# Gated cross-attention and a low-rank expert layer: the first two key groups by context blocks, in a new order of loads, with zeros in front

## What is computed

```python
x = x + tanh(g_xattn) * xattn(layernorm(x), ctx, ...)
x = x + tanh(g_ffn) * ffn(layernorm(x), ...)

# xattn(text, features)
features_n = rmsnorm(features, fn_w)
Q = rmsnorm(text @ Wq_w.T + Wq_b, qn_w)
K = rmsnorm(features_n @ Wk_w.T + Wk_b, kn_w)
attn = softmax(Q @ K.T / sqrt(1024))
attended = attn @ features_n

# ffn(x)
base = x @ W_base.T + b_base
w = normalized part of softmax(x @ W_gate.T) above its threshold
moe = 2.0 * sum over experts e of w_e * (x @ A_e.T) @ B_e.T
```

## Time and profile before

| | us |
|---|---|
| median of 3 executions | 489.45 (488.79 to 489.53) |
| the profiled execution | 489.19 |
| its span, first to last instruction | 487.1 |
| TensorE busy | 473.6 (97%) |
| VectorE busy | 345.9 (71%) |
| ScalarE busy | 164.6 (34%) |
| GpSimd busy | 127.5 (26%) |

### The profile page before, as it was taken

The page is one execution under the profiler, slowest core; times in us unless marked ns, Lnnn a source line. Parts: engine busy times, 40 slices in busy tenths (PEclk is TensorE's granted clock), DMA queues, the critical chain, the costliest instruction groups (busy, mean ns, idle before and its releaser), DMA issues.

```text
span 487.1 us, 6840 instructions
## 1 busy us (share of the span) xinstructions
PE 473.6 (97%) x2460; PEld 402.2 (83%) x2460; DVE 345.9 (71%) x720; ACT 164.6 (34%) x338; POOL 127.5 (26%) x113
## 2 busy tenths in 40 slices
PE   4999999999999999999999999999999999999997
PEld 3888899998888888888888887877888888888885
DVE  1267758563787867769977996988767679777742
ACT  3765312310214204227326325244151422414300
POOL 1011011002353353336152515514040401305000
PEclk9999999999999999999999999999999999999999
DMA  8962262027843368557669035040503113050202
GB/s 291 412 247 87 88 250 96 1 87 253 266 137 123 150 215 283 199 200 249 208 257 399 4 131 215 27 146 2 172 3 129 45 60 113 1 173 1 86 0 87
DMA packets 20160, 71.80 MB, mean 147 GB/s; under 512 B 2464, under 2 KB 3488, under 8 KB 18848
## 3 DMA queue, kind: packets, MB, share of 16 engines
q1 hardware_dynamic: 19984, 71.35, 40.8%
q10 hardware_dynamic: 144, 0.02, 0.0%
HBM read 56.69 MB, written 14.68 MB: 147 GB/s over the span
## 4 chain that ended last, share of the span: by engine, by line
PE 79%; DVE 11%; issue 4%; DMA 3%; ACT 2%; POOL 0%; SPq 0%; DVEq 0%; ACTq 0%; POOLq 0%
PE bank L706 8%; PE bank L710 8%; PE bank L708 8%; PE bank L558 6%; PE bank L623 6%; PE bank L625 6%; PE bank L624 6%; PE bank L588 3%; PE bank L590 3%; PE bank L589 3%; PE bank L686 3%; PE bank L487 2%; DVE wl_T L1316 2%; DMA out_dram<-xs 2%; PE bank L609 2%
## 5 line engine op out<-in xcount | busy, mean ns | idle before, releaser
L1430 POOL TENSOR_TENSOR small<-small,tiny 128x1 f32<-128x1 f32 (+2 forms) x25 | 23.6, 945 | 150.3 <-DVE small L1079 124.1
L623 PE MATMUL bank<-xth,gram 128*128 128x512 f32 x144 | 57.4, 398 | 0.0
L625 PE MATMUL bank<-xtl,gram 128*128 128x512 f32 x144 | 56.3, 391 | 0.0
L624 PE MATMUL bank<-xth,gram 128*128 128x512 f32 x144 | 56.1, 390 | 0.0
L1404 DVE SCALAR_TENSOR_TENSOR xs<-bank,tiny,xs 128x512 f32<-128x512 f32 x56 | 40.2, 747 | 21.6 <-PE bank L710 15.7
L706 PE MATMUL bank<-wh_B,zh 128*128 128x512 f32 x136 | 55.2, 406 | 0.0
L710 PE MATMUL bank<-wh_B,zl 128*128 128x512 f32 x136 | 53.5, 393 | 0.0
L708 PE MATMUL bank<-wl_B,zh 128*128 128x512 f32 x136 | 53.3, 392 | 0.0
L1458 POOL TENSOR_TENSOR sq_sum<-sq_sum,sq 128x512 f32<-128x512 f32 x24 | 32.0, 1332 | 62.7 <-DVE sq L1252 62.7
L1494 POOL TENSOR_TENSOR xs<-xs,bb 128x1024 f32<-128x1024 f32 x16 | 39.5, 2468 | 10.3 <-ACT zn L946 7.7
L706 PE MATMUL bank<-wh_T,zh 128*128 128x512 f32 x96 | 39.3, 410 | 1.8 <-DVE wl_T L1316 1.6
(11 more groups left out here) (185 smaller groups left out, 1111.5 us busy)
## 6 DMA issues: line engine op xcount, KB each, us to landing
xst<-x_dram SPq DMA_DIRECT2D x16, 512.0 KB, 3.6
xz<-xt_dram SPq DMA_DIRECT2D x16, 512.0 KB, 6.8
out_dram<-xs SPq DMA_DIRECT2D x14, 512.0 KB, 3.0
xa<-x_dram SPq DMA_DIRECT2D x12, 512.0 KB, 3.3
x<-xa SPq DMA_DIRECT2D x12, 512.0 KB, 2.6
xs<-x SPq DMA_DIRECT2D x12, 512.0 KB, 4.0
wq_raw<-wq_dram SPq DMA_DIRECT2D x8, 512.0 KB, 14.9
wr_B<-wb_dram SPq DMA_DIRECT2D x4, 1024.0 KB, 8.5
```

The lines of the kernel that those rows point to most:

```text
L623: pe.matmul(acc[:, :], gram[:, g, 0, :], xth[b % 2][:, r, :], start=r == ROWS[j][0], stop=False)
L624: pe.matmul(acc[:, :], gram[:, g, 1, :], xth[b % 2][:, r, :], start=False, stop=False)
L625: done = pe.matmul(acc[:, :], gram[:, g, 0, :], xtl[b % 2][:, r, :], start=False, stop=r == ROWS[j][-1])
```

## The change

In front of its stages VectorE writes zeros into a tile `idle` of 258 columns, and TensorE waits for them and issues five fp32 matmuls of 128x256 on them, into bank 7, whose contents are overwritten later. ScalarE issues an activation of one column of `idle`, ahead of its first stage. A stage `k01` takes the place of k(0) and k(1): it goes over the eight blocks of `ct` and issues the product of each block for group 0 and group 1 in turn. The weights of both groups land in four loads of two blocks for both groups (256 KB, in rows of 1 KB), each behind the piece of `ct` that it belongs to. The other loads and the stages are put into another order: k(2) comes ahead of g(0,0), the ctx loads behind wq1 and wk3, wq1 ahead of wk3. A stage of `g` issues the high by high products of all its pieces first, then high by low, then low by high; in sweep 0 it waits for the high parts (`a_wq`) at its start and for the low parts (`v_wq`) ahead of the second of these passes. A bank now signals in the third pass. Nothing of the arithmetic is left out.

```diff
-        first = [..., ("key_bias",), ("k", 0), ("k", 1), ("wq", 0), ("wq", 1),
-                 ("g", 0, 0), ("ctx_norm",), ("k", 2), ("wq", 2), ("rsb",), ("g", 0, 1), ("k", 3), ("wq", 3),
-                 ("k_out", 0), ("k_out", 1), ("k_low", 0), ("k_low", 1), ("g", 0, 2), ("k_out", 2), ("k_out", 3), ("k", 4),
...
+        first = [..., ("key_bias",), ("k01",), ("wq", 0), ("wq", 1),
+                 ("k", 2), ("g", 0, 0), ("ctx_norm",), ("wq", 2), ("k", 3), ("rsb",), ("g", 0, 1), ("k_out", 0), ("k_out", 1),
+                 ("wq", 3), ("k_low", 0), ("k_low", 1), ("g", 0, 2), ("k_out", 2), ("wq", 4), ("k_out", 3), ("k", 4),
+                 ("k_low", 2), ("k_low", 3), ("g", 0, 3), ("x_stat", 0), ("wq", 5), ("k", 5), ("x_stat", 1), ("g", 0, 4),
+                 ("wq", 6), ("k_out", 4), ("k_out", 5), ("k_low", 4), ("k_low", 5), ("wq", 7), ("g", 0, 5), ("x_stat", 2),
+                 ("g", 0, 6), ("x_stat", 3), ("g", 0, 7), ("k", 6), ("k", 7), ("g_out", 0), ("load_xt", 0),
...
+            pe.wait_ge(v_idle, 1)
+            for n in range(IDLE):
+                pe.matmul(bank[T_BANKS[0]][:, 0:2 * P], idle[:, 0:P], idle[:, 0:2 * P], start=True, stop=True)
...
+                elif stage == "k01":
+                    for c in range(KB):
+                        if c % CK == 0:
+                            pe.wait_ge(ld_wk01[c // CK], 16)
+                        pe.wait_ge((a_ct, v_ct)[c % 2], c // 2 + 1)
+                        for f in range(2):
+                            done = pe.matmul(k_at(f), wk01[:, f, c, :], ct[:, c, :], start=f == c == 0, stop=c == KB - 1,
+                                             skip_group_check=True)
...
-                    if sweep == 0:
-                        pe.wait_ge(v_wq, f + 1)
-                    for n_bank, pieces in SWEEPS[sweep]:
...
-                            pe.matmul(dst, wqh[f][:, a], wh_c, start=n == f == 0, stop=False, skip_group_check=True)
-                            pe.matmul(dst, wqh[f][:, a], wl_c, start=False, stop=False, skip_group_check=True)
-                            done = pe.matmul(dst, wql[f][:, a], wh_c, start=False, stop=f == FB - 1, skip_group_check=True)
+                    for left, right in ((0, 0), (0, 1), (1, 0)):
+                        if sweep == left == 0:
+                            pe.wait_ge(*((v_wq, f + 1) if right else (a_wq, f + 1)))
+                        for n_bank, pieces in SWEEPS[sweep]:
...
+                                done = pe.matmul(dst, blocks[left][:, row, :],
+                                                 blocks[right][:, cols.start:cols.stop:cols.step, :],
+                                                 start=n == f == left == right == 0, stop=left == 1 and f == FB - 1,
+                                                 skip_group_check=True)
...
-            load_ct(0)
-            sp.dma_start(wkf[0][:, 0:4, :], wk[0][:, 0:4, :]).then_inc(ld_wk[0], 16)
-            sp.dma_start(wkf[0][:, 4:8, :], wk[0][:, 4:8, :]).then_inc(ld_wk0, 16)
-            load_ct(1)
-            load_ct(2)
-            load_ct(3)
-            load_wk(1)
+            for c in range(4):
+                kc = slice(CK * c, CK * c + CK)
+                load_ct(c)
+                sp.dma_start(wk01[:, :, kc, :], wk[0:2].rearrange("f p c m -> p f c m")[:, :, kc, :]).then_inc(ld_wk01[c], 16)
+            load_wk(2)
             load_wq(0)
+            load_wq(1)
+            load_wk(3)
             load_ctx(0)
             load_ctx(1)
-            load_wk(2)
-            load_wq(1)
-            load_wk(3)
             load_wq(2)
+            load_wk(4)
+            load_wq(3)
             load_x(0)
             load_x(1)
-            for f in range(4, FB):
+            for f in range(5, FB):
                 load_wk(f)
                 load_wq(f - 1)
...
+            act.wait_ge(v_idle, 1)
+            act.activation(idle[:, 2 * P:2 * P + 1], idle[:, 2 * P + 1:2 * P + 2], ACT.Copy)
...
+            dve.memset(idle[:, :], 0.0).then_inc(v_idle, 1)
```

More of the change, by code:

```diff
@@ L125, in build @@
         ct = at("ct", [P, KB, S_ALL], F32, r_x0)
+        wk01 = at("wk01", [P, 2, KB, P], F32, r_wk[0])
         wkf = [at(f"wkf{f}", [P, KB, P], F32, o) for f, o in enumerate(r_wk)]
@@ L212, in build @@
         s_top, s_nb, s_sum, s_rec = (small[:, k:k + TPB] for k in (44, 48, 52, 56))
+        idle = at("idle", [P, 2 * P + 2], F32, r_z)
         x1_dram = nc.dram_tensor("x1", [(NT - TPB) * P, D], F32)
@@ L235, in build @@
         ld_xt = [sem(f"ld_xt{i}") for i in range(4)]
-        ld_wk0 = sem("ld_wk0b")
         ld_ctx = [sem(f"ld_ctx{i}") for i in range(2)]
@@ L239, in build @@
         ld_wk = [sem(f"ld_wk{i}") for i in range(FB)]
+        ld_wk01 = ld_wk[0:2] + [sem(f"ld_wk01_{c}") for c in range(2)]
         ld_wq = [sem(f"ld_wq{i}") for i in range(FB)]
@@ L249, in build @@
             sem(f"p_{n}") for n in ("ring", "k", "g", "m", "mr", "y", "s", "hd", "prod", "fin"))
+        v_idle = sem("v_idle")
         p_first, a_first, v_first = (sem(f"{n}_first") for n in "pav")
@@ L265, in build @@
         CONSTS = 8
+        IDLE = 5
         PLAIN_PRODUCTS = [("11a", "a11", "B11", "A", True), ("11b", "a12", "B21", "A", False),
@@ L326, in build @@
                     free.append((z_slot[p, z], ("prod", p, n)))
-        first = [("ct", 0), ("ct", 1), ("ct", 2), ("ct", 3), ("small",), ("key_bias",), ("k", 0), ("k", 1), ("wq", 0), ("wq", 1),
-                 ("g", 0, 0), ("ctx_norm",), ("k", 2), ("wq", 2), ("rsb",), ("g", 0, 1), ("k", 3), ("wq", 3),
-                 ("k_out", 0), ("k_out", 1), ("k_low", 0), ("k_low", 1), ("g", 0, 2), ("k_out", 2), ("k_out", 3), ("k", 4),
-                 ("k_low", 2), ("wq", 4), ("k_low", 3), ("g", 0, 3), ("x_stat", 0), ("k", 5), ("wq", 5), ("x_stat", 1),
-                 ("g", 0, 4), ("k_out", 4), ("k_out", 5), ("k_low", 4), ("wq", 6), ("k_low", 5), ("g", 0, 5), ("x_stat", 2),
-                 ("wq", 7), ("g", 0, 6), ("x_stat", 3), ("g", 0, 7), ("k", 6), ("k", 7), ("g_out", 0), ("load_xt", 0),
+        first = [("ct", 0), ("ct", 1), ("ct", 2), ("ct", 3), ("small",), ("key_bias",), ("k01",), ("wq", 0), ("wq", 1),
[3 rows of a table added]
+                 ("wq", 6), ("k_out", 4), ("k_out", 5), ("k_low", 4), ("k_low", 5), ("wq", 7), ("g", 0, 5), ("x_stat", 2),
+                 ("g", 0, 6), ("x_stat", 3), ("g", 0, 7), ("k", 6), ("k", 7), ("g_out", 0), ("load_xt", 0),
                  ("k_out", 6), ("k_out", 7), ("k_low", 6), ("k_low", 7), ("g", 1, 0), ("x_stat", 4), ("g", 1, 1),
@@ L546, in tensor @@
                     transposes(acc, px[:, :, :].bitcast(F32))
+                elif stage == "k01":
[6 more added lines that the diff above has]
+                                             skip_group_check=True)
+                            if c == KB - 1:
+                                done.then_inc(p_k, 1)
                 elif stage == "k":
@@ L550, in tensor @@
                         pe.wait_ge(v_kr, f - 2)
-                    if f > 0:
-                        pe.wait_ge(ld_wk[f], 16)
+                    pe.wait_ge(ld_wk[f], 16)
                     for c in range(KB):
[L554 to L557, removed]
                         done = pe.matmul(k_at(f), wkf[f][:, c, :], ct[:, c, :], start=c == 0, stop=c == KB - 1,
@@ L575, in tensor @@
                     sweep, f = i
-                    if sweep == 0:
-                        pe.wait_ge(v_wq, f + 1)
-                    for n_bank, pieces in SWEEPS[sweep]:
[L579 to L587, removed]
-                            pe.matmul(dst, wqh[f][:, a], wh_c, start=n == f == 0, stop=False, skip_group_check=True)
-                            pe.matmul(dst, wqh[f][:, a], wl_c, start=False, stop=False, skip_group_check=True)
-                            done = pe.matmul(dst, wql[f][:, a], wh_c, start=False, stop=f == FB - 1, skip_group_check=True)
-                        if f == FB - 1:
-                            done.then_inc(p_g, 1)
@@ new lines, in tensor @@
+                    blocks = [w[f][:, :].rearrange("p (c d) -> p c d", d=P) for w in (wqh, wql)]
+                    for left, right in ((0, 0), (0, 1), (1, 0)):
+                        if sweep == left == 0:
+                            pe.wait_ge(*((v_wq, f + 1) if right else (a_wq, f + 1)))
+                        for n_bank, pieces in SWEEPS[sweep]:
+                            if sweep == 1 and f == left == right == 0 and n_bank == 5:
+                                pe.wait_ge(v_kr, 6)
+                            elif sweep == 1 and f == left == right == 0:
+                                pe.wait_ge(v_gl, [n for n, _ in SWEEPS[0]].index(n_bank) + 1)
+                            for n, (row, cols, off) in enumerate(pieces):
+                                dst = bank[n_bank][:, off * P:(off + len(cols)) * P].rearrange("p (c d) -> p c d", d=P)
+                                done = pe.matmul(dst, blocks[left][:, row, :],
```

(5 more changed lines are left out.)

## The result

| | before | changed |
|---|---|---|
| median, us | 489.27 (488.74 to 490.19, 6 executions) | 486.44 (486.12 to 486.94, 6) |
| ratio | | 0.9943, 95% interval 0.9931 to 0.9955 |
| the profiled execution, us | 489.19 | 486.12 |
| its span, us | 487.1 | 484.2 |

A forecast was written before the change was run, and what follows sets the result against it. TensorE, busy 473.6 of 487.1 us, was taken as the bound, so only its start and matmul rate count. Terms -1.29 - 1.62 - 0.09 + 0.2 = -2.8 us gave 486.4 profiled, 486.6 median; range 485.8 to 488.3.

The forecast's parts named there:

- Table load, -1.29: Before the first product: the early dummy activation takes ScalarE's table load out of the chain, TensorE starting at 5.80, -1.29 us.
- Clock, -1.62: First key products: ten zero instructions raise TensorE's clock beforehand, so seven slow instructions run at full pace, -1.62 us.
- Rival (a): Zeros fail before the first product: clock still low at 5.80, or falls back in the gap; 487.5 to 488.2 us, chance 0.20.
- if the clock rises as long after the first zero as it did after the first product (3.1 us): Block of zeros: the clock would rise at 4.2 us and the zeros end at 4.8, 1.0 us before the products.
- at worst they delay nothing: Block of zeros: even at 0.44 us each, the ten instructions fill 1.1 to 5.5 us, before the start at 5.80.
- Waits in k01, +0.1 of the 0.2: Stage k01: TensorE waits 0.1 us for pair 4's weights; with the other joints 0.2 us in the sum.
- pair 2 with the fourth 256 KB at 6.8: Loads for k01: the second pair of context blocks is complete at 6.8 us, counted at the old queue's places.
- Pairs 3 and 4: Loads for k01: third and fourth pairs of context blocks complete at 9.0 and 10.5 us, the fourth with 0.3 us slack.
- rival (b): Weight pieces in 1 KB rows hold k01: 488.7 us at half rate, 487.4 at half that slip; chance 0.10.
- The price of 1 KB rows, +0.4 us for 1 MB: Loads of wk01: 1 KB rows cost 15% more time per byte, +0.4 us, making pair 4 complete at 10.9 us.
- The order behind it: After k01: k(2) ends at 16.0 us, g(0,0) waits at most 0.1 us for wql, and rsb is covered.
- Carrying to the end: From the start through the VectorE-bound stretch after 220 us: nothing is tied to absolute time, so the gain arrives in full.

The follow-up runs named there:

- four blocks: The changed kernel with ct and wk01 each loaded in two pieces of four blocks (four transfers of 512 KB instead of eight of 256 KB): 489.32 us, ratio 0.9991.
- ScalarE's queue: The changed kernel with the four wk01 weight pieces issued by ScalarE behind vecs instead of by SyncE between the ct pieces: 490.43 us, ratio 1.0021.
- front alone: The kernel before with only the matmuls of zeros and ScalarE's early activation added; loads, k(0), k(1) and g as they were: 488.92 us, ratio 0.9992.

## Why the prediction was right, point by point

- **Table load, -1.29.** Right in its mechanism; the start came at 5.52 instead of 5.80, because vecs landed 0.28 us earlier in this execution (the activation began at 4.87, not 5.15). That is luck and not the edit: vecs also landed earlier, at 4.83 and 4.92 us instead of 5.07, in the two kernels that keep the old loads. By itself the edit measures 0.9 us, because without it the pieces have more time to land.
- **Clock, -1.62.** Right: all 32 products at the full clock in the profiled execution, and the kernel without zeros 1.6 us slower. Rival (a) is out as the rule, though not for every execution: with the old order inside g, which changes nothing ahead of it, the rise came at 6.66 and three products were slow. And I gave the margin wrongly: "if the clock rises as long after the first zero as it did after the first product (3.1 us)". It took 3.2 to 5.8 us (below). In five of the nine traces with five zeros or more they were slow to the tenth instruction, which fills TensorE until 5.6 us; with the old order inside g this delayed a first product that could have begun at 5.4, and with 2 KB rows, where vecs landed first of all, the zeros held it from 4.9 to 5.3. So "at worst they delay nothing" is off by 0.2 to 0.4 us.
- **Waits in k01, +0.1 of the 0.2.** This term was mis-sized: 0.3 us. The step that failed is "pair 2 with the fourth 256 KB at 6.8". I counted bytes at the places of the old queue; the same fourth place landed at 7.43. Pairs 3 and 4, which I watched, were in time: 3.13 + 5.7 = 8.8 and 4.12 + 6.2 = 10.3 against 9.0 and 10.5. And it was not the 1 KB rows, my rival (b): 2 KB rows changed nothing.
- **The price of 1 KB rows, +0.4 us for 1 MB.** About right as a price, and without effect, since pairs 3 and 4 were early. By the packets, 1 MB in rows of 1 KB holds each of the 16 DMA engines for 64 x 46 ns = 2.9 us, and in rows of 4 KB for 16 x 159 ns = 2.5 us. The sentence of the Trainium skill that I set against my row (DMA: Bandwidth & Descriptors, Specifications, line rate from 512 B on) came to the right total, since nothing waited for these bytes, but these traces don't bear it out: 22 bytes per ns on one engine at 1 KB, 24 at 2 KB and 26 at 4 KB.
- **The order behind it.** k(2) ended and g(0,0) began at 16.02, forecast 16.0 (partly by luck: with 6.72 us for k01 the forecast left out 0.2 us that the earlier start made good); k(6) began at 53.09, forecast 53.3. The second pass of g(0,0) did not wait for wql0, which was ready at 16.5, and rsb cost nothing.
- **Carrying to the end.** Right; twenty zeros show it with the opposite sign.

In the traces the start is 7.09 - 5.52 = 1.57 us earlier, the seven slow steps cost 3.11 - 7 x 0.216 = 1.60, and the waits in k01 are +0.33: together -2.8. So two misses cancelled, a start 0.3 us earlier than forecast and waits somewhat longer, but they hang together. By the landings of this trace a start at 5.80 would have wanted pair 2 at about 7.6 and found it there at 7.43; k01 would then have ended at 12.8 all the same (an estimate from these landings and steps).

## What to carry to other kernels

An engine that is busy to the end can be sped up by starting it earlier, but only if every supplier of its first 20 us moves too: here a ready engine alone and an earlier supply alone gained nothing, and both together 2.8 us. To make the first real matmuls run at the full clock, give TensorE work on data that needs no load from the first instant on. Here five matmuls of zeros, some 4 to 4.6 us, had the clock up ahead of the first product in six of eight traces, also with 1.8 us of rest between, and within its first four instructions in the other two; two matmuls with 2.2 us of rest behind them did nothing. A block that is sized to end just ahead of the first product can also delay it by a few tenths. Count landings of small pieces from a trace of that queue order, not by bytes from another.

## What the runs showed of the hardware

**The clock's rise scatters.** From the first matmul of a block to the rise, us. The rise is where the trace's record of the granted clock begins; where matmuls run at that moment, their step falls from 0.43 to 0.22 us there. (Ahead of that record the column of the granted clock shows 1.00 though the steps are those of the low clock.)

| block | from | rise at | us |
|---|---|---|---|
| products, kernel before | 7.09 | 10.18 | 3.1 |
| products, high parts first alone | 6.94 | 9.77 | 2.8 |
| products, loads and orders alone | 6.78 | 9.69 | 2.9 |
| products, no zeros | 5.42 | 9.00 | 3.6 |
| products, behind two zeros and a gap of 2.2 us | 5.42 | 8.31 | 2.9 |
| zeros and products, change (two profiles) | 1.19 | 4.82, 4.36 | 3.6, 3.2 |
| the same, 2 KB rows; four blocks | 1.19 | 4.94, 5.07 | 3.8, 3.9 |
| the same, no early activation; ScalarE's queue | 1.19 | 5.84, 6.54 | 4.6, 5.3 |
| the same, old g; twenty zeros; front alone | 1.19 | 6.66, 6.84, 6.99 | 5.5, 5.6, 5.8 |

Zeros raise the clock as other data do. With the old order inside g and with the front edits alone the rise came only among the products, and the first three or four of them were slow. A rest of 0.9 us (no early activation) or 1.8 us (four blocks, ScalarE's queue) behind the zeros did not lower the clock; on ScalarE's queue the rise even falls into the rest, 0.7 us after the last zero ended. The scatter agrees with what the Trainium skill says of it (TensorE: Matmul & The Clock Gate, What's actually happening: it differs from run to run). It would also explain why executions without full zeros differ by some 2 us (487.5 to 489.6 without zeros) and those of the change by 0.8; that was not tested by itself.

**A slow microsecond of the DMA.** In all traces with ct and wk01 in turn, whatever the rows and the number of pieces, the DMA moves 140 to 206 GB/s for a microsecond at 5 to 7 us (210 and 272 over two with ScalarE's queue), and 311 or more with the old order. It doesn't come from the zeros: the kernels without them have it (140 and 175 GB/s), and the one with zeros and the old loads doesn't. What in the order causes it stays open.

**Two queues share.** A queue that runs ahead takes bandwidth from the transfers that are wanted first: a 256 KB piece issued at 2.70 us on ScalarE's queue took 12.4 us; the same piece, the last of the four, took 6.2 us in the change.

**Packets by size.** 1 KB 46 ns, 2 KB 84 ns, 4 KB 159 ns (medians of the packets up to 12 us), so a byte in rows of 1 KB costs 9% more than in rows of 2 KB and 16% more than in rows of 4 KB.
